# A chunked recurrence on one core: the second chunk's part moved across the tile boundary, with a new order of work on every engine

## What is computed

```
def step(s, inp):
    q_, w_, k_, v_, a_, b_ = inp
    sa = jnp.einsum('bhij,bhj->bhi', s, a_)
    s = s * w_[:, :, None, :] + sa[..., None] * b_[:, :, None, :] + v_[..., None] * k_[:, :, None, :]
    return (s, jnp.einsum('bhij,bhj->bhi', s, q_))
```

## Time and profile before

| | us |
|---|---|
| median of 3 runs | 3132.63 |
| lowest and highest | 3129.85, 3137.59 |
| the profiled execution, its own time | 3138.99 |
| its span, from first to last instruction | 3137.3 |

### The profile page before, as it was taken

The page is one execution under the profiler, slowest core; times in us unless marked ns, Lnnn a source line. Parts: engine busy times, 40 slices in busy tenths (PEclk is TensorE's granted clock), DMA queues, the critical chain, the costliest instruction groups (busy, mean ns, idle before and its releaser), DMA issues.

```text
span 3137.3 us, 175510 instructions
## 1 busy us (share of the span) xinstructions
PE 2873.8 (92%) x80064; PEld 2523.7 (80%) x80128; DVE 2807.0 (89%) x5699; ACT 1672.6 (53%) x3334; POOL 1420.0 (45%) x1224
## 2 busy tenths in 40 slices
PE   5899999999999999999999999999999999999995
PEld 5788788888887887888888888888888888888874
DVE  4898899999999998999999999999999899889985
ACT  3464555555554654655655655555555545546552
POOL 5344444444444444444444444444444444444442
PEclk9999999999999999999999999999999999999997
DMA  4121221222222222212212212212222222222121
GB/s 132 40 64 40 57 53 45 64 50 49 62 50 47 64 50 47 64 44 54 64 43 55 64 43 55 56 45 60 53 48 61 50 47 64 50 48 64 42 49 39
DMA packets 92603, 170.68 MB, mean 54 GB/s; under 512 B 13908, under 2 KB 14932, under 8 KB 91864
## 3 DMA queue, kind: packets, MB, share of 16 engines
q1 hardware_dynamic: 91864, 159.45, 21.7%
HBM read 41.97 MB, written 16.78 MB: 19 GB/s over the span
## 4 chain that ended last, share of the span: by engine, by line
PE 87%; DVE 7%; issue 5%; SPq 1%; DMA 0%; ACT 0%; POOL 0%; POOLq 0%; ACTq 0%; DVEq 0%
PE bank L1100 31%; PE bank_a L1239 12%; PE bank L1300 8%; PE bank L1107 4%; PE bank_a L1217 4%; PE bank_b L1217 4%; DVE stacked L939 4%; PE bank_a L1270 3%; PE bank_b L1270 3%; PE bank_a L1247 3%; PE bank_a L1255 3%; PE bank_b L1290 2%; PE bank_a L1290 2%; PE bank L1182 2%; DVE xm_k L816 2%
## 5 line engine op out<-in xcount | busy, mean ns | idle before, releaser
L1239 PE MATMUL bank_a<-pw,w_ffn_int 32*32 32x64 f32 x16384 | 273.0, 216 | 37.9 <-issue 33.2
L420 POOL TENSOR_TENSOR xm_wa<-xm_wa,xT 128x512 f32<-128x512 f32 x64 | 75.4, 1178 | 500.4 <-DVE xm_wa L816 500.4
L1239 PEld LDWEIGHTS bank_a<-pw,w_ffn_int 32*32 32x32 f32 x16384 | 242.3, 105 | 66.3 <-issue 53.2
L1100 PE MATMUL bank<-xm_rg,w_r 128*128 128x128 f32 x2048 | 285.7, 282 | 3.1 <-issue 3.1
L1100 PE MATMUL bank<-xm_v,w_v 128*128 128x128 f32 x2048 | 269.1, 279 | 4.6 <-issue 3.1
L527 ACT ACTIVATE pw<-bank_a 128x512 f32<-128x512 f32 x192 | 114.6, 597 | 287.2 <-PE bank_a L1239 286.7
L1100 PEld LDWEIGHTS bank<-xm_rg,w_r 128*128 128x128 f32 x2048 | 249.9, 192 | 15.4 <-issue 3.9
L1300 PE MATMUL bank<-w_o,yc 128*128 128x512 f32 x512 | 251.2, 614 | 11.3 <-DVE yc L781 10.3
L1100 PEld LDWEIGHTS bank<-xm_v,w_v 128*128 128x128 f32 x2048 | 245.1, 192 | 13.5 <-issue 7.7
L1100 PE MATMUL bank<-xm_k,w_k 128*128 128x128 f32 x2048 | 240.8, 276 | 2.0 <-issue 2.0
L1100 PEld LDWEIGHTS bank<-xm_k,w_k 128*128 128x128 f32 x2048 | 235.5, 193 | 2.2 <-issue 2.2
(11 more groups left out here) (198 smaller groups left out, 8334.3 us busy)
## 6 DMA issues: line engine op xcount, KB each, us to landing
streamed<-aq_state SPq DMA_DIRECT2D x128, 384.0 KB, 5.3
streamed<-w_ffn_int SPq DMA_DIRECT2D x128, 384.0 KB, 5.3
xin<-in_x SPq DMA_DIRECT2D x128, 128.0 KB, 4.8
xres<-in_x SPq DMA_DIRECT2D x128, 128.0 KB
out<-o_sb SPq DMA_DIRECT2D x128, 128.0 KB, 2.4
w_ffn_int<-in_weight_q SPq DMA_DIRECT2D x1, 2048.0 KB, 9.7
w_k<-in_Wk SPq DMA_DIRECT2D x1, 1024.0 KB
w_r<-in_Wr SPq DMA_DIRECT2D x1, 1024.0 KB
```

The lines of the kernel that those rows point to most:

```text
L420: return nc.gpsimd.tensor_tensor(out_, in0, in1, ALU.add)
L1100: ins = mm(bank[:, o * n:(o + 1) * n], weights[:, k, o * P:(o + 1) * P], x[:, k].rearrange("p b t -> p (b t)"), start=(k == 0), stop=(k == ...
L1239: ins = mm(bank_a[q, 64 * n:64 * n + 64], pt[q, g, :], source[q, g, 0:2].rearrange("p j t -> p (j t)"), start=True, stop=True)
```

## The change

Chunk 1's five steps leave the `solve` part of a tile and stand in the `finish` part of the next `tile_step`: on TensorE `from_values_and_state(n, 1)` is the first thing in the step, before the keys' projection and the scores of the next tile; `solve_step(n, 1)` follows `scores_b(m)` and `from_solutions(n, 1)` follows the gates. Both chunks now work in bank_b, so chunk 1 waits for the copy of chunk 0's output. `scores_k(m)`, which overwrites bank_b, moves behind `power(m, 1)`. `first` gets two more planes so that the next tile's scores don't overwrite what chunk 1 still reads. ScalarE's copy of the queries goes, and VectorE reads them from their PSUM bank. `gn_rstd` shares storage with `yc` instead of `rn`. The order of the pieces is new on POOL, ACT, DVE and PE; SP's is as it was.

```diff
-        r_raw = sb("r_raw", [P, G, CHUNK])
-        first = sb("first", [P, G, 4, CHUNK])
+        first = sb("first", [P, 6, G, CHUNK])
-        gn_rstd = rn
+        gn_rstd = yc
-        def step_bank(c):
-            return (bank_b, bank_a)[c]
-
-        def step_part(c, part):
-            return step_bank(c)[:].rearrange("p (g j t) -> p g j t", j=4, t=CHUNK)[:, :, part, :]
+        def step_part(part):
+            return bank_b[:].rearrange("p (g j t) -> p g j t", j=4, t=CHUNK)[:, :, part, :]
...
-            def queries(i):
-                act.wait_ge(p_r, count(i, 1, 1))
-                act.wait_ge(v_q, count(i, 1, 0))
-                run(r_raw[:], fb[2][:].rearrange("p (g t) -> p g t", t=CHUNK), ACT.Copy).then_inc(a_r, 1)
...
-                dve.wait_ge(a_r, count(i, 1, 1))
-                tt(aq[:, 1], r_raw[:], pdec[:, :, 1:], ALU.mult).then_inc(v_q, 1)
+                dve.wait_ge(p_r, count(i, 1, 1))
+                tt(aq[:, 1], by_chunk(fb[2]), pdec[:, :, 1:], ALU.mult).then_inc(v_q, 1)
...
                 if c == 1:
-                    pe.wait_ge(v_t, count(m, 1, 1))
+                    pe.wait_ge(a_y, count(m, NC, 1))
```

More of the change, by code:

```diff
@@ L714, in tile_step @@
                 if project:
-                    mk_gate(i)
-                    squares(i)
+                    key_decay(i)
                 if solve:
-                    power(m, 0)
+                    output_gate(m)
                 if project:
[L720 to L726, removed]
-                if mix:
[L728 to L745, removed]
+                    tables(SIGMOID_TANH)
+                    gate_hidden(i)
+                if mix:
                     low_rank(j)
@@ L1011, in tile_step @@
                     scores_b(m)
+                    bonus_rows(m)
+                if project:
+                    removal_keys(i)
+                if mix:
+                    norm_input(j)
+                if finish:
+                    update_state(n, 1)
+                if solve:
+                    power(m, 0)
                 if finish:
@@ L1035, in tile_step @@
                 if solve:
-                    bonus_sums(m)
+                    token_major_keys(m)
+                if project:
+                    decayed(i)
+                if solve:
                     power(m, 2)
@@ L1284, in from_solutions @@
             def from_solutions(m, c):
-                bank = step_bank(c)
+                bank = bank_b
+                own = 2 + 2 * (m % 2)
                 if c == 0:
@@ L1290, in from_solutions @@
                     ins = mm(bank[q, 4 * CHUNK * j + CHUNK:4 * CHUNK * j + 3 * CHUNK], both(u2[q, j]),
-                             first[q, g, 2:4].rearrange("p j t -> p (j t)"), start=False, stop=True,
+                             first[q, own:own + 2, g], start=False, stop=True,
                              skip_group_check=True)
@@ L1325, in tile_step @@
                     scores_b(m)
+                if finish:
+                    solve_step(n, 1)
                 if project:
                     gates(i)
+                if finish:
+                    from_solutions(n, 1)
+                if solve:
+                    power(m, 0)
+                if project:
+                    decay_gate(i)
+                    values(i, [0])
+                    queries(i, [0])
+                    queries(i, [1])
+                if solve:
+                    power(m, 1)
+                if project:
+                    values(i, [1])
+                    values(i, [2])
                 if solve:
@@ L1359, in tile_step @@
                 if solve:
+                    half_inverse(m)
+                    output_gate(m)
                     from_values_and_state(m, 0)
-                    inverse(m)
                 if mix:
                     low_rank(j)
-                if project:
-                    gate_hidden(i)
                 if solve:
-                    solve_step(m, 0)
-                    output_gate(m)
-                    from_solutions(m, 0)
+                    inverse(m)
                 if mix:
```

191 lines of the change are left out of this document (99 added, 92 removed).

## The result

The changed kernel takes 3349.6 us (median of 4 runs, 3345.2 to 3354.6), against 3135.1 us before in the same session: a ratio of 1.067, 95% interval 1.065 to 1.070. Forecast was 3230 us in a range from 3071 to 3330. The direction was right, the size was not: +214 us where +98 was worked out. The profiled execution has a span of 3343.5 us.

The account below looks back on a forecast made before the run. TensorE, 92% busy, was taken as the bound, with VectorE near at 89%. To the profiled 3139 us it added 24 for waits and 74 for instruction fetch: 3237, or 3231 by the median, forecast 3230 us, range 3071 to 3330.

Parts of the forecast that it names:

- both named waits: TensorE's waits for chunk 0's state (54.2 us) and chunk 1's right-hand sides (19.5 us); removal forecast at -71 us.
- The wait at from_solutions(m, 0): After solve_step, TensorE stands still while ScalarE copies the solution, output_gate no longer between: +1.03 us a tile.
- The second wait: At from_values(n, 1), TensorE waits for VectorE's state update and ScalarE's copy of output 0: 0.5 us a tile.
- a debt of 3.5 us a tile at most: Instruction fetch falling behind in two denser stretches, 1.9 + 1.6 us; a third taken, 1.2 us a tile, +74 us.
- stretch (A): scores_b through power: 640 instructions want 8.2 us of fetch against 6.9 us of work, short by 1.3 us.
- (B): half_inverse to from_solutions(m, 0): 864 instructions want 11.1 us of fetch against 9.8 us of work, short by 1.3 us.
- Rival 1: Fetch as before: blocks in hand cover the denser stretches, only waits count, 3157 us; chance 0.17.
- rival 2: Faster: fetch goes on during the new waits and the 86.0 us of issue gaps vanish, 3071 us; chance 0.22.
- Rival 3: Keys land late: from_values(m, 0) waits some 1 us a tile for their transfer, 3292 us; chance 0.10.
- each tile about 49.2 us: The forecast's time per tile in the changed kernel, going with 3230 us, 3% slower; before, a tile took 47.6 us.
- VectorE's total stays: Among the small parts priced at nothing: VectorE's total time is unchanged and below the new period.

## Why the prediction was wrong

**The waits.** Removed: forecast 71 us, and both named waits went. The wait at from_solutions(m, 0): forecast 1.03 us a tile, found 1.03 in the tile and 68.5 us in all. The second wait, for the output's copy, was forecast at 0.5 us a tile; it is 3.7 us in all. Its chain was even longer than worked out (q_bf 1.28 instead of 0.43), but TensorE's own work ahead of it, priced at 5.9 us, ran at the low clock and covered it. The trace shows both sides: where the clock was low between from_solutions and from_values (54 cases) the wait is 0.02 us on average, where it was full (11 cases) 0.30 us. TensorE's waits on other engines came out 2 us over those of before instead of 24.

**Fetch.** Forecast +74 us from a debt of 3.5 us a tile at most, of which a third was taken. The issue gaps grew by 72 us. That is the right size; the third was a choice, and its agreement is partly luck. The cause is shown by the runs with the inverse doubled and halved, and by the gaps' distances in instructions and from the queue's transfers. How it divides between the two stretches is less clear than the prediction had it: gaps moved from one to another when solve_step was taken out of stretch (A), while half the inverse taken out of (B) removed more than half of the difference. What remains, 32 us, was not traced. Rival 1 (fetch as before) and rival 2 (fetch fills the waits) are refuted: the gaps grew. Rival 3 did not occur, no wait for the keys' transfer is in the view.

**The step that failed is "each tile about 49.2 us", the sum itself: it held every work time fixed at its row of before.** The clock is a term that it left out. The prediction used 5.9 us for TensorE's work behind mixed_inputs, 9.8 and 6.9 us for the stretches, as if idle time cost its length only. TensorE's busy time grew by 127 us, as the time at 1.2 GHz went from 82 to 361 us. The filler runs show the cause for a part: work laid into the bare wait gave back 50 us while no other wait was shortened but that one. The trace of before had it, at a place that the prediction did not read:

```profile
287.87 0.43 PE L1255 MATMUL bank_a<-pw,w_ffn_int 32*32 32x16 f32 x30 [1.99 <-issue]
288.23 1.25 PE L1100 MATMUL bank<-xn,w_maa 128*128 128x128 f32 x8
289.27 1.92 PE L1100 MATMUL bank<-xm_rg,w_gate 128*128 128x128 f32 x8
```

Behind an issue gap of 1.99 us in the kernel before, gate_hidden takes 1.92 us where eight such matmuls take 1.05 in the earlier trace rows; the granted clock from 287.80 to 291.20 was 0.70. A forecast of more gaps should have carried this as a term, bounded by the work behind each gap at nearly twice its price.

**VectorE's total.** "VectorE's total stays" failed too: +150 us, of which 160 us lie in three instructions that meet GpSimd's. The order of pieces on one engine was costed as neutral; it also sets what runs beside what. Removing the collisions gave back about 32 us, and that run's order is another one too.

What the 214 us are made of, from the runs: fetch gaps 72 us directly; 127 us of busy time at the lower clock; and a few us of other idle. The collisions work through both. Of the clock's part, the filler measures what can be had at the bare wait. The trace's record of the granted clock has 76 low stretches, 366 us in all (361 by the mean): 41 of them, 167 us, have an issue gap and the bare wait in the 7 us ahead of them (again a distance chosen for the count), 27, 130 us, have issue gaps alone, and 8 have others or are the ramps. That the issue gaps caused the 130 us is argued from this order in time; the doubled inverse, whose added gaps took the clock from 0.987 to 0.942, bears it out.

What was not tried: moving chunk 1's recurrence alone with the old order of everything else. The shared bank and the dependencies of every engine's list force most of the new order, so a single cause for the whole loss was not isolated in this way.

## What to carry to other kernels

Count instructions, not only time, in front of a reordering: a stretch of small matmuls that wants 256 instructions in less than the 3.3 to 3.8 us seen here tends to be paid in gaps, and pieces with few instructions are its cover. Idle time on TensorE has a second price in the clock, so a wait should not be put next to gaps that are there already. An order that is written by hand on every engine must also be checked for what VectorE newly starts while GpSimd runs.

## What the runs showed of the hardware that was not expected

- 256 more instructions in a dense stretch cost 5.0 us a tile, with 1.2 us of work in them; 16 instructions with 1.0 us of work cost 0.8 us.
- Issue gaps lie whole blocks of 256 instructions apart (124 of 127 intervals before, 152 of 167 after), and nine in ten end 2.1 to 2.8 us after the start of a 16,384-byte transfer of the instruction queue. Two such starts are never less than 3.2 us apart.
- The clock fell behind issue gaps that are, between the ramps, at most 2.9 us long each, and it did not fall for two gaps of 1.0 us with 2.3 us of matmuls between them. Filler matmuls raised it from 0.946 to 0.971. Two kernels with nearly the same idle time, 332.8 and 342.3 us, had 0.986 and 0.946.
- The VectorE instructions x2n, q_bf and kt, on SBUF operands, end after the GpSimd operation of 1.2 to 1.6 us beneath which they start: 0.43 becomes 1.28 us, 0.70 becomes 1.66. Where GpSimd starts second, VectorE's bt keeps 0.68 us and GpSimd's operation goes from 1.18 to 1.56. An operation that reads one operand from PSUM kept its time.
